# Side work spread over more gaps and over ScalarE, and one GpSimd addition made in two

## The chip, the cores and the metric
The kernel runs on one core of one Trainium2 chip. The metric is the device time of one execution in microseconds; the median of three runs of the kernel before is 1218.67 us (1215.61 to 1218.83).

## The reference, cut to what matters
Eight sequences of 512 tokens and 256 features go through a linear attention layer with a Taylor feature map, a residual and a layer norm, and then through a top-1 router with eight experts of width 1024 (GELU), a residual and a layer norm. All is float32.

```python
def taylor_exp(x):                       # 16 features -> 1 + 16 + 256
    x2 = (x[..., :, None] * x[..., None, :]).reshape(*x.shape[:-1], FD * FD) / R2
    return jnp.concatenate([jnp.ones_like(x[..., :1]), x / RRD, x2 / RD], axis=-1)
# 16 heads; q, k, v from x; k_enc, v_enc from the first 128 tokens
A_qk = jnp.tril(einsum('bhnd,bhmd->bhnm', taylor_exp(q), taylor_exp(k)))
y1 = einsum('bhnm,bhme->bhne', A_qk, v)
y2 = einsum('bhnm,bhme->bhne', einsum('bhnd,bhmd->bhnm', q_f, k_enc_f), v_enc)
z = 1.0 / ((q_f * k_state).sum(-1) + EPS)       # the row sum of the weights
x = layernorm(x + ((y1 + y2) * z) @ Wout.T)
# then: top-1 expert of softmax(x @ wr + br), gate, gelu(x @ w1 + b1) @ w2 + b2
x = layernorm(x + moe(x))
```

The weight of a query and a key is (s + sqrt(1/2))^2 + 1/2 of the scaled dot product s, so that one square and one addition of a half stand for the feature map.

## The kernel before, in words
The function `attention` handles the eight sequences (batches) one after the other, and each batch as eight pairs of heads. A pair has four units: the score blocks of unit 0 (encoder keys), 1, 2 and 3 (the causal key tiles). A batch is therefore 32 gaps, numbered g = 0 to 31, and each engine runs its own hand-written order over the gaps; semaphores tie them together.

In gap g with unit u = g % 4, for pair n = 8b + g // 4:

- TensorE multiplies the scores of pair n + 1, unit u (`scores`, L725, into two PSUM slots), then weighs the values of pair n with the finished weights of unit u (`weigh`, L746), in unit 3 also sums the row sums of the weights (`denominators`, L759). After that it does at most one *piece*, side work for the batch before or after, into the single PSUM bank `piece`: a V projection (L622, `V_LATE_AT` for the second half of this batch's values, `V_EARLY_AT` for the first half of the next batch's), a query or key projection for the next batch (`QK_AT`, five of them), an output projection of the batch before (`OUT_AT`, four, L669), the two turns of the normalised rows (`TURN_AT`, L705) and the router (`ROUTER_AT`, L712). A piece waits until the reader of the one ahead has emptied the bank (`piece_read`).
- ScalarE first copies the piece of gap g - 1 if it is a V piece (L392) or the high part of a QK piece (L404), then squares the scores (L379); in unit 0 it also adds a half (L384) and copies the attention output of the last pair (L412).
- VectorE first makes the low part of a QK piece (L482) or adds the residual (L530, L532) for the piece of gap g - 1, then finishes the weights of unit u of pair n + 1: a masked multiply (L490, for units 1 to 3) and an addition of a half to the rest (L493, called half-add below). Behind that stands its side work by gap number: the inversion of the row sums (gap 1, L497), the split of the next batch's x into a high part `xh` (gap 6, L470) and a low part `xl` (gap 7, L474), eight normalisations of the last batch's attention output (gaps 8 to 15, L502), moments (25, L537), centring (27, L542), the copies of the turned rows (L548) and the router's logits (L553).
- GpSimd adds the finished weights of the pair's blocks for the row sums: one addition of 2 x 512 columns after unit 1 (L339), one of 2 x 384 and one of 2 x 128 after unit 2 (L342, L345), one of 2 x 256 after unit 3 (L349). In gap 26 it makes `rstd` (L354, L357), for which the centring waits.
- SyncE's queue holds all loads and stores in a fixed order. It sends the high and low parts of q and k to DRAM (`send`, L209 to L218), gathers them as operands of two pairs (`gather`, L226, L229), stores the inverse row sums (L241), loads them spread over the partitions (`load_inverse`, L252, two pairs each), stores the rows (L257) and loads x.

The first projection of the next batch (`project_qk`, i = 0) waits for both parts of x (`x_split`); output projection 0 waits for all eight normalisations; turn 0 waits for all centred rows (`y_ready`). `experts` runs after the attention.

Of the kernel before, what the change touches and what calls it, by code (L numbers as in the profile page):

```python
# [11 lines left out]
ALU = mybir.AluOpType  # L12
# [26 lines left out]
V_LATE_AT = {0: 0, 1: 1, 2: 2, 3: 3, 4: 4}  # L39
QK_AT = {9: 0, 11: 1, 13: 2, 15: 3, 17: 4}  # L40
OUT_AT = {18: 0, 20: 1, 22: 2, 24: 3}
V_EARLY_AT = {19: 0, 21: 1, 23: 2, 25: 3, 27: 4}
TURN_AT, ROUTER_AT = {29: 0, 30: 1}, 31
XH_GAP, XL_GAP = 6, 7
INVERT_GAP, NORM_GAP, MOMENTS_GAP, CENTRE_GAP, RSTD_GAP = 1, 8, 25, 27, 26
# [53 lines left out]
def attention(nc, sem, xT_in, x_in, wqk_in, wv_in, wo_in, wr_in, br_in, ybuf, inv_rows, k_rows, q_rows,  # L99
              logits, ident, tables):  # L100
    falling, tile_starts, count128, before, ones, ones32 = tables
    with ExitStack() as ctx:
# [80 lines left out]
        def _(sp):  # L183
# [89 lines left out]
            for b in range(B):  # L273
                if b + 1 < B:
                    load_x(b + 1)
                if b > 0:
                    store_inverse(b - 1)
                gather(b, 2)
                if b > 0:
                    for g in range(PAIRS // 2):  # L280
                        load_inverse(b - 1, g)
                gather(b, 3)
                if b + 1 < B:
                    send(b + 1, 0)
                    gather(b + 1, 0)
                    send(b + 1, 1)
                if b > 0:
                    store_rows(b - 1)
                if b + 1 < B:
                    gather(b + 1, 1)  # L290
                if b > 0:
                    load_rows(b)
# [4 lines left out]
        def _(pool):  # L297
# [34 lines left out]
            def add_blocks(n, u):  # L332
                src, dst = w[:, n % 2, :, :], wsum[:, n % 2, :, :]
                pool.wait_ge(w_ready, FIXES * n + FIXED[u])
                if u == 1:
# [3 lines left out]
                    pool.tensor_tensor(dst, src[:, :, 0:N], src[:, :, N:2 * N], ALU.add).then_inc(wsummed, 1)  # L339
# [32 lines left out]
        def _(act):  # L372
# [32 lines left out]

            def copy_att(n):
                act.wait_ge(weighed, UNITS * (n + 1))
                if n == 0:
                    act.wait_ge(w_split, 22)
                if n >= ATT:  # L410
                    act.wait_ge(piece_full, nth((n - ATT) // PAIRS, "out", NT - 1) + 1)
                act.activation(att[:, n % ATT, :], osum[n % 2][:, :], ACT.Copy).then_inc(att_copied, 1)  # L412
# [19 lines left out]
            for b in range(B):  # L432
                for g in range(GAPS):
# [5 lines left out]
                    if b + 1 < B and g - 1 in V_EARLY_AT:  # L439
                        copy_values(b + 1, 0, V_EARLY_AT[g - 1])  # L440
                    if b * PAIRS + p + 1 < B * PAIRS:
# [6 lines left out]
            copy_att(B * PAIRS - 1)  # L448

        @block.vector  # L450
        def _(dve):
# [15 lines left out]
            def split_x_high(b):  # L467
                dve.wait_ge(xT_loaded, 16 * (b + 1))
                dve.wait_ge(piece_full, nth(b - 1, "v", 9) + 1)
                dve.tensor_copy(xh[:, :, :], xT[:, :, :]).then_inc(x_split, 1)  # L470

            def split_x_low(b):
# [72 lines left out]
            def copy_turned(b, k):  # L545
                dve.wait_ge(piece_full, nth(b, "turn", k) + 1)
                bank = osum[1] if b == B - 1 and k == 1 else piece
                dve.tensor_copy(yT[:, 4 * k:4 * k + 4, :],  # L548
                                bank[:, :].rearrange("p (t n) -> p t n", n=P)).then_inc(piece_read, 1)

# [25 lines left out]
            for b in range(B):  # L576
                for g in range(GAPS):
# [5 lines left out]
                    if b > 0 and g - 1 in TURN_AT:  # L583
                        copy_turned(b - 1, TURN_AT[g - 1])
                    if b > 1 and g == 0:
                        logits_of(b - 2)
                    if n < B * PAIRS and u > 0:
                        finish_weights(n, u)
                    if b + 1 < B and g == XH_GAP:
                        split_x_high(b + 1)  # L590
# [4 lines left out]
                    if b > 0 and 0 <= g - NORM_GAP < PAIRS:  # L595
                        normalise((b - 1) * PAIRS + g - NORM_GAP)
# [4 lines left out]
            logits_of(B - 2)  # L601
# [11 lines left out]
            copy_turned(B - 1, 0)  # L613
            copy_turned(B - 1, 1)
# [664 lines left out]
```

## Time and profile before
| | us |
|---|---|
| median of the runs | 1218.67 |
| the profiled execution, its own time | 1217.28 |
| its span | 1215.5 |
| TensorE busy | 1080.9 (89%) |
| VectorE busy | 627.7 (52%) |
| ScalarE busy | 495.5 (41%) |
| GpSimd busy | 592.4 (49%) |
| attention phase, to the last batch's row sums | about 798 |
| expert phase, to the end | about 417 |

The page of a profile gives busy time by engine, then 40 slices of the span, then groups of instructions by line. A share over the whole span says little here, as the two phases have different limits; the timelines of single stretches and the list of who waited for whom say more. "Idle before" in a timeline row is the time in which the engine had nothing to do ahead of that row, with what ended it. The granted clock is a share of 2.4 GHz; 0.50 is 1.2 GHz, and a value between is a mix of both over the stretch.

### The profile page before, as it was taken

Reading aid. Unit: us, or ns where it says so; the run is one execution under the profiler, and the core shown is the slowest. Engines: PE = TensorE matmul, PEld = TensorE weight load, DVE = VectorE, ACT = ScalarE, POOL = GpSimd, SP = SyncE. Lnnn points to the kernel's source line nnn. Section 1 sums busy time; section 2 is a strip of 40 time slices with the busy share of each in tenths; the row PEclk is TensorE's granted clock in tenths of the full one; section 3 lists DMA queues with packets and bytes.
Section 4 is the critical chain, followed back from the end, with each engine's and each line's share of the span. In section 5 each row is a group of like instructions: output and inputs, shape, how many; then the busy total and the mean of one; then the engine's idle time right before and its main releaser. Section 6 shows DMA issues by size and latency. Waiting matters only on the chain. (4 is left out here: it accounts for less than half of the span.)

```text
span 1215.5 us, 16762 instructions
## 1 busy us (share of the span) xinstructions
PE 1080.9 (89%) x5296; PEld 629.5 (52%) x5297; DVE 627.7 (52%) x986; ACT 495.5 (41%) x868; POOL 592.4 (49%) x571
## 2 busy tenths in 40 slices
PE   5789899999989989989998998883479999999994
PEld 4344455445436445445544543463357766677663
DVE  5476864583492574466448349646423334343342
ACT  2557554544553454454454455300023233332331
POOL 1467755573574565456457357500124544444442
PEclk9789999999999899999999998976589999999998
DMA  6635352443534235235244343014551000111010
GB/s 205 249 108 183 92 193 83 142 152 118 155 120 161 92 114 218 102 91 184 85 150 148 122 131 92 1 35 169 226 237 33 31 33 29 34 35 31 25 31 2
DMA packets 54110, 134.90 MB, mean 111 GB/s; under 512 B 5854, under 2 KB 10176, under 8 KB 51746
## 3 DMA queue, kind: packets, MB, share of 16 engines
q1 hardware_dynamic: 50306, 124.81, 29.7%
q0 software_dynamic: 3744, 9.31, 2.5%
q8 instruction: 35, 0.57, 0.2%
q14 instruction: 25, 0.20, 0.1%
HBM read 87.73 MB, written 47.29 MB: 111 GB/s over the span
## 5 line engine op out<-in xcount | busy, mean ns | idle before, releaser
L379 ACT ACTIVATE w<-slot 128x1024 f32<-128x1024 f32 (+1 forms) x256 | 233.4, 915 | 176.3 <-PE slot L725 173.6
L339 POOL TENSOR_TENSOR wsum<-w 128x1024 f32<-128x1024 f32 x64 | 158.9, 2483 | 258.6 <-DVE w L493 258.6
L490 DVE SCALAR_TENSOR_TENSOR w<-w,mask 128x256 f32<-128x256 f32 (+1 forms) x192 | 192.9, 1005 | 169.6 <-ACT w L379 158.9
L746 PE MATMUL osum<-w,values 128*64 128x512 f32 (+3 forms) x1280 | 264.1, 511 | 2.0 <-DVE w L493 1.9
L342 POOL TENSOR_TENSOR wsum<-wsum,w 128x768 f32<-128x768 f32 x64 | 126.6, 1978 | 59.6 <-DVE w L493 59.6
L1156 ACT ACTIVATE active<-upT,b 128x128 f32<-128x128 f32 x312 | 84.9, 383 | 158.4 <-PE upT L1234 158.4
L1210 PE MATMUL down<-w,active 128*128 x624 | 144.2, 385 | 2.5 <-ACT active L1156 2.5
L1222 PE MATMUL up<-w,rowsT 128*128 x312 | 143.3, 603 | 0.7 <-ACT rowsT L1145 0.7
L725 PE MATMUL slot<-qop,kop 64*128 64x512 f32 (+3 forms) x640 | 130.2, 438 | 10.5 <-issue 8.3
L493 DVE TENSOR_SCALAR w<-w 128x768 f32<-128x768 f32 (+2 forms) x192 | 138.8, 723 | 0.0
L1210 PEld LDWEIGHTS down<-w,active 128*128 128x128 f32 x624 | 117.6, 193 | 18.7 <-issue 3.8
L725 PEld LDWEIGHTS slot<-qop,kop 64*128 64x128 f32 x640 | 58.0, 195 | 132.1 <-issue 118.6
L349 POOL TENSOR_TENSOR wsum<-wsum,w 128x512 f32<-128x512 f32 x64 | 93.6, 1463 | 25.5 <-DVE w L493 24.0
L669 PE MATMUL piece<-wo,att 128*128 128x256 f32 x448 | 104.2, 385 | 1.6 <-DVE att L502 1.6
L669 PEld LDWEIGHTS piece<-wo,att 128*128 128x128 f32 x448 | 82.8, 190 | 31.5 <-ACT values L392 9.7
L746 PEld LDWEIGHTS osum<-w,values 128*64 128x64 f32 x1280 | 68.7, 142 | 57.0 <-issue 44.2
L1187 DVE COPY inner<-up 128x1024 f32<-128x1024 f32 x39 | 47.7, 1223 | 91.2 <-PE up L1222 91.2
L392 ACT ACTIVATE values<-piece 128x512 f32<-128x512 f32 x75 | 44.9, 598 | 113.3 <-PE piece L622 113.3
L1222 PEld LDWEIGHTS up<-w,rowsT 128*128 128x128 f32 x312 | 57.3, 194 | 58.8 <-issue 58.7
L1170 DVE TENSOR_TENSOR result<-down,b 128x256 f32<-128x256 f32 x39 | 16.6, 424 | 114.8 <-PE down L1210 87.3
L530 DVE TENSOR_TENSOR y<-piece,y 128x256 f32<-128x256 f32 x28 | 11.9, 424 | 115.2 <-PE piece L669 115.2
L384 ACT ACTIVATE w<-w 128x1024 f32<-128x1024 f32 x64 | 67.7, 1058 | 2.0
(186 smaller groups left out, 1215.9 us busy)
## 6 DMA issues: line engine op xcount, KB each, us to landing
kop<-k_rows SPq DMA_DIRECT2D x32, 640.0 KB, 4.7
qop<-q_rows SPq DMA_DIRECT2D x32, 512.0 KB, 5.9
w<-in_w SPq DMA_DIRECT2D x16, 1024.0 KB, 9.5
inv<-inv_rows SPq DMA_DIRECT2D x56, 256.0 KB, 5.7
k_rows<-kh SPq DMA_DIRECT2D x32, 320.0 KB
k_rows<-kl SPq DMA_DIRECT2D x32, 320.0 KB
q_rows<-qh SPq DMA_DIRECT2D x32, 256.0 KB
q_rows<-ql SPq DMA_DIRECT2D x32, 256.0 KB
```

Of the source, the lines that this page charges most:

```text
L339: pool.tensor_tensor(dst, src[:, :, 0:N], src[:, :, N:2 * N], ALU.add).then_inc(wsummed, 1)
L342: pool.tensor_tensor(dst[:, :, P:N], dst[:, :, P:N], src[:, :, 2 * N + P:3 * N], ALU.add).then_inc(wsummed, 1)
L349: pool.tensor_tensor(dst[:, :, 2 * P:N], dst[:, :, 2 * P:N], src[:, :, 3 * N:WIDTH], ALU.add).then_inc(wsummed, 1)
L379: act.activation(w[:, n % 2, :, at:at + cols], slot[u % 2][:, :, 0:cols], ACT.Square, bias=HALF_ROOT).then_inc(squared, 1)
L490: dve.scalar_tensor_tensor(src[:, :, 0:cut], src[:, :, 0:cut], 0.5, mask[:, 0:cut].unsqueeze(1).to_broadcast([P, 2, cut]), ALU.add, ALU.mu ...
L493: dve.tensor_scalar(src[:, :, cut:], src[:, :, cut:], 0.5, None, ALU.add).then_inc(w_ready, 1)
L669: last = pe.matmul(piece[:, 0:D], att[:, (b * PAIRS + p) % ATT, t * P:t * P + P], wo[:, p, :], start=(p == 0), stop=(p == PAIRS - 1))
L725: last = pe.matmul(slot[u % 2][:, s, col:col + N - q0], kop[HD * s:HD * s + HD, n % RING, j * P:j * P + P], qop[HD * s:HD * s + HD, n % RI ...
L746: last = pe.matmul(osum[n % 2][HD * s:HD * s + HD, q0:N], values[:, j, h * HD:h * HD + HD], w[:, n % 2, s, at:at + N - q0], start=(u == 0) ...
L1156: act.activation(active[:, k % 2, c, :], upT[:, c * P:(c + 1) * P], ACT.Gelu, bias=b1[:, bass.ds(e * IC + c, 1)]).then_inc(active_ready, 1)
L1210: last = pe.matmul(down[k % 2][:, :], active[:, k % 2, c, :], w2[:, bass.ds(e, 1), c, :].rearrange("p o d -> p (o d)"), start=(c == 0), st ...
L1222: last = pe.matmul(up[:, h * 512:(h + 1) * 512], rowsT[:, k % 2, c, :], w1[:, bass.ds(e, 1), c, h * 512:(h + 1) * 512].rearrange("p o d -> ...
```

## The change
The gaps of most pieces move. V pieces of this batch run in gaps 0, 1, 3, 5, 6; QK pieces in 10, 12, 14, 25, 27; outputs in 15, 17, 19, 21; V pieces of the next batch in 16, 18, 20, 22, 24; turns in 26 and 28; the router in 30. The normalisations go by a table, into gaps 4, 5, 6, 7, 9, 10, 12, 13; `xh` to gap 7 and `xl` to 8; moments to 22, `rstd` to 23, centring to 24. The split of `xh` and the two copies of turned rows move from VectorE to ScalarE, ahead of its square of the same gap. The logits are read in gap 31, not at the start of the next batch. In SyncE's queue two of the four inverse loads now stand ahead of the gather of pairs 4 and 5, and the store of the rows stands ahead of the second `send`. GpSimd's addition of 2 x 512 columns (L339) becomes two of 512, one for each head; the second one signals.

```diff
--- before.py
+++ after.py
@@ -36,13 +36,14 @@
 UNIT_AT, UNIT_COLS = [0, 512, 1024, 1536], [512, 512, 512, 256]
 FIXED, FIXES = [0, 2, 4, 6], 6
 RING, ATT, INV = 4, 14, 4
-V_LATE_AT = {0: 0, 1: 1, 2: 2, 3: 3, 4: 4}
-QK_AT = {9: 0, 11: 1, 13: 2, 15: 3, 17: 4}
-OUT_AT = {18: 0, 20: 1, 22: 2, 24: 3}
-V_EARLY_AT = {19: 0, 21: 1, 23: 2, 25: 3, 27: 4}
-TURN_AT, ROUTER_AT = {29: 0, 30: 1}, 31
-XH_GAP, XL_GAP = 6, 7
-INVERT_GAP, NORM_GAP, MOMENTS_GAP, CENTRE_GAP, RSTD_GAP = 1, 8, 25, 27, 26
+V_LATE_AT = {0: 0, 1: 1, 3: 2, 5: 3, 6: 4}
+QK_AT = {10: 0, 12: 1, 14: 2, 25: 3, 27: 4}
+OUT_AT = {15: 0, 17: 1, 19: 2, 21: 3}
+V_EARLY_AT = {16: 0, 18: 1, 20: 2, 22: 3, 24: 4}
+TURN_AT, ROUTER_AT = {26: 0, 28: 1}, 30
+XH_GAP, XL_GAP = 7, 8
+NORM_AT = {4: 0, 5: 1, 6: 2, 7: 3, 9: 4, 10: 5, 12: 6, 13: 7}
+INVERT_GAP, MOMENTS_GAP, CENTRE_GAP, RSTD_GAP = 1, 22, 24, 23
 COPY_UNIT, DEN_UNIT = 0, 3
 QH = N // 2
 
@@ -275,18 +276,21 @@
                     load_x(b + 1)
                 if b > 0:
                     store_inverse(b - 1)
+                if b > 0:
+                    for g in range(2):
+                        load_inverse(b - 1, g)
                 gather(b, 2)
                 if b > 0:
-                    for g in range(PAIRS // 2):
+                    for g in range(2, PAIRS // 2):
                         load_inverse(b - 1, g)
                 gather(b, 3)
                 if b + 1 < B:
                     send(b + 1, 0)
                     gather(b + 1, 0)
-                    send(b + 1, 1)
                 if b > 0:
                     store_rows(b - 1)
                 if b + 1 < B:
+                    send(b + 1, 1)
                     gather(b + 1, 1)
                 if b > 0:
                     load_rows(b)
@@ -336,7 +340,8 @@
                     pool.wait_ge(enc_ready, n + 1)
                     if n >= 2:
                         pool.wait_ge(den_full, n - 1)
-                    pool.tensor_tensor(dst, src[:, :, 0:N], src[:, :, N:2 * N], ALU.add).then_inc(wsummed, 1)
+                    pool.tensor_tensor(dst[:, 0, :], src[:, 0, 0:N], src[:, 0, N:2 * N], ALU.add)
+                    pool.tensor_tensor(dst[:, 1, :], src[:, 1, 0:N], src[:, 1, N:2 * N], ALU.add).then_inc(wsummed, 1)
                 elif u == 2:
                     pool.wait_ge(wsummed, 4 * n + 1)
                     pool.tensor_tensor(dst[:, :, P:N], dst[:, :, P:N], src[:, :, 2 * N + P:3 * N],
@@ -402,6 +407,17 @@
                 bank = first_bank[i] if b == 0 else piece[:, :]
                 src = bank[:, 0:2 * P].rearrange("p (m n) -> p m n", m=2) if i == 2 else bank
                 act.activation(dst, src, ACT.Copy, scale=CQ if i in (0, 3) else 1.0).then_inc(qk_hi, 1)
+
+            def split_x_high(b):
+                act.wait_ge(xT_loaded, 16 * (b + 1))
+                act.wait_ge(piece_full, nth(b - 1, "v", 9) + 1)
+                act.activation(xh[:, :, :], xT[:, :, :], ACT.Copy).then_inc(x_split, 1)
+
+            def copy_turned(b, k):
+                act.wait_ge(piece_full, nth(b, "turn", k) + 1)
+                bank = osum[1] if b == B - 1 and k == 1 else piece
+                act.activation(yT[:, 4 * k:4 * k + 4, :], bank[:, :].rearrange("p (t n) -> p t n", n=P),
+                               ACT.Copy).then_inc(piece_read, 1)
 
             def copy_att(n):
                 act.wait_ge(weighed, UNITS * (n + 1))
@@ -438,6 +454,10 @@
                         high_qk(b + 1, QK_AT[g - 1])
                     if b + 1 < B and g - 1 in V_EARLY_AT:
                         copy_values(b + 1, 0, V_EARLY_AT[g - 1])
+                    if b > 0 and g - 1 in TURN_AT:
+                        copy_turned(b - 1, TURN_AT[g - 1])
+                    if b + 1 < B and g == XH_GAP:
+                        split_x_high(b + 1)
                     if b * PAIRS + p + 1 < B * PAIRS:
                         square(b * PAIRS + p + 1, u)
                         if u == 0:
@@ -446,6 +466,8 @@
                         copy_att(b * PAIRS + p - 1)
                 copy_den(b)
             copy_att(B * PAIRS - 1)
+            copy_turned(B - 1, 0)
+            copy_turned(B - 1, 1)
 
         @block.vector
         def _(dve):
@@ -464,12 +486,8 @@
                 dve.wait_ge(w_split, 6 + 2 * (4 * c + n) + 1)
                 dve.tensor_tensor(lo, src, hi.bitcast(F32), ALU.subtract).then_inc(w_split, 1)
 
-            def split_x_high(b):
+            def split_x_low(b):
                 dve.wait_ge(xT_loaded, 16 * (b + 1))
-                dve.wait_ge(piece_full, nth(b - 1, "v", 9) + 1)
-                dve.tensor_copy(xh[:, :, :], xT[:, :, :]).then_inc(x_split, 1)
-
-            def split_x_low(b):
                 dve.wait_ge(x_split, 2 * b + 1)
                 dve.tensor_tensor(xl[:, :, :], xT[:, :, :], xh[:, :, :].bitcast(F32), ALU.subtract).then_inc(x_split, 1)
 
@@ -541,12 +559,6 @@
                 for t in range(NT):
                     dve.tensor_scalar(y[:, t, :], y[:, t, :], mv[:, t, 0:1], rstd[:, t:t + 1], ALU.subtract,
                                       ALU.mult).then_inc(y_ready, 1)
-
-            def copy_turned(b, k):
-                dve.wait_ge(piece_full, nth(b, "turn", k) + 1)
-                bank = osum[1] if b == B - 1 and k == 1 else piece
-                dve.tensor_copy(yT[:, 4 * k:4 * k + 4, :],
-                                bank[:, :].rearrange("p (t n) -> p t n", n=P)).then_inc(piece_read, 1)
 
             def logits_of(b):
                 dve.wait_ge(piece_full, nth(b, "router", 0) + 1)
@@ -580,25 +592,20 @@
                         low_qk(b + 1, QK_AT[g - 1])
                     if b > 0 and g - 1 in OUT_AT:
                         residual(b - 1, OUT_AT[g - 1])
-                    if b > 0 and g - 1 in TURN_AT:
-                        copy_turned(b - 1, TURN_AT[g - 1])
-                    if b > 1 and g == 0:
-                        logits_of(b - 2)
+                    if b > 0 and g - 1 == ROUTER_AT:
+                        logits_of(b - 1)
                     if n < B * PAIRS and u > 0:
                         finish_weights(n, u)
-                    if b + 1 < B and g == XH_GAP:
-                        split_x_high(b + 1)
                     if b + 1 < B and g == XL_GAP:
                         split_x_low(b + 1)
                     if b > 0 and g == INVERT_GAP:
                         invert(b - 1)
-                    if b > 0 and 0 <= g - NORM_GAP < PAIRS:
-                        normalise((b - 1) * PAIRS + g - NORM_GAP)
+                    if b > 0 and g in NORM_AT:
+                        normalise((b - 1) * PAIRS + NORM_AT[g])
                     if b > 0 and g == MOMENTS_GAP:
                         moments(b - 1)
                     if b > 0 and g == CENTRE_GAP:
                         centre(b - 1)
-            logits_of(B - 2)
             invert(B - 1)
             pick(0)
             pick(1)
@@ -610,8 +617,6 @@
                 residual_last(t)
             moments(B - 1)
             centre(B - 1)
-            copy_turned(B - 1, 0)
-            copy_turned(B - 1, 1)
             logits_of(B - 1)
 
         @block.tensor
```

## Rows read from the trace of the kernel before
**Rows 1.** The page, part 1: busy time, share of the span, instructions.
```profile
PE 1080.9 (89%) x5296; PEld 629.5 (52%) x5297; DVE 627.7 (52%) x986; ACT 495.5 (41%) x868; POOL 592.4 (49%) x571
```
**Rows 2.** Waits of TensorE, 0 to 760 us: us in total, times, longest.
```profile
PE piece L622 <- DVE xl L474: 22.6, 7, 4.0
PE piece L705 <- DVE y L542: 11.5, 6, 1.9
...
PE piece L622 <- DVE ql L482: 8.1, 6, 1.4
```
**Rows 3.** Timeline of TensorE, 340 to 410 us: start, duration, what, [idle before, releaser].
```profile
342.17 0.70 PE L622 MATMUL piece<-xh,wqk_h 128*128 128x512 f32 x2 [3.09 <-DVE xl L474]
...
363.12 0.74 PE L622 MATMUL piece<-xh,wqk_h 128*128 128x512 f32 x2 [1.36 <-DVE ql L482]
...
406.80 0.63 PE L705 MATMUL piece<-ident,y 128*128 128x128 f32 x4 [1.92 <-DVE y L542]
```
**Rows 4.** Windows, one batch: length, busy by engine, granted clock, DMA share, GB/s.
```profile
412.95:512.39 99.44, 93.05 (x490) 49.01 (x490) 56.19 (x85) 48.95 (x65) 54.77 (x35) 0.95 0.39 132
```
**Rows 5.** Windows behind four idle times of TensorE, same columns.
```profile
342.00:348.00 6.00, 5.83 (x32) 2.90 (x32) 5.80 (x8) 2.22 (x3) 3.90 (x2) 0.72 0.26 78
363.00:369.00 6.00, 5.88 (x31) 4.23 (x32) 3.35 (x6) 1.52 (x2) 4.21 (x3) 1.00 0.53 209
506.00:512.00 6.00, 5.78 (x35) 2.92 (x36) 4.56 (x8) 1.62 (x2) 4.08 (x2) 0.72 0.84 284
512.00:518.00 6.00, 6.00 (x27) 3.76 (x28) 1.30 (x3) 2.95 (x4) 2.15 (x3) 0.72 0.45 176
```
**Rows 6.** Timeline of TensorE: a V piece, gaps without pieces, an output piece.
```profile
330.12 0.73 PE L622 MATMUL piece<-wv_h,xh 128*128 128x512 f32 x2
...
331.72 0.50 PE L725 MATMUL slot<-qop,kop 64*128 64x512 f32 x2
...
337.57 0.50 PE L725 MATMUL slot<-qop,kop 64*128 64x512 f32 x2
...
382.55 3.72 PE L669 MATMUL piece<-wo,att 128*128 128x256 f32 x16
```
**Rows 7.** Timeline of VectorE, 334 to 344 us.
```profile
334.81 2.44 DVE L490 SCALAR_TENSOR_TENSOR w<-w,mask 128x512 f32<-128x512 f32 x1 [0.55 <-ACT w L379]
...
338.12 2.04 DVE L490 SCALAR_TENSOR_TENSOR w<-w,mask 128x256 f32<-128x256 f32 x1
...
340.81 1.21 DVE L474 TENSOR_TENSOR xl<-xT,xh 128x1024 fp32r<-128x1024 f32 x1
341.94 1.77 DVE L502 TENSOR_TENSOR att<-att,inv 128x512 f32<-128x512 f32 x1
```
**Rows 8.** Timeline of GpSimd, 328 to 344 us.
```profile
328.38 1.28 POOL L349 TENSOR_TENSOR wsum<-wsum,w 128x512 f32<-128x512 f32 x1 [0.23 <-DVE w L493]
334.35 2.36 POOL L339 TENSOR_TENSOR wsum<-w 128x1024 f32<-128x1024 f32 x1 [4.69 <-DVE w L493]
...
340.97 2.20 POOL L349 TENSOR_TENSOR wsum<-wsum,w 128x512 f32<-128x512 f32 x1 [0.23 <-DVE w L493]
```
**Rows 9.** SyncE's timeline; then DMA issues: KB, us to landing, 340:346 and 327.5:329.4.
```profile
323.73 1.30 SPq L241 DMA_DIRECT2D inv_rows<-den_sb  x4
...
327.09 26.16 SPq L252 DMA_DIRECT2D inv<-inv_rows  x8
...
inv<-inv_rows SPq DMA_DIRECT2D x2, 256.0 KB, 3.7
...
inv<-inv_rows SPq DMA_DIRECT2D x4, 256.0 KB, 7.7
```
**Rows 10.** Timeline of ScalarE: a 1024-column square.
```profile
339.17 1.02 ACT L379 ACTIVATE w<-slot 128x1024 f32<-128x1024 f32 x1
```
**Rows 11.** Timeline of VectorE: the centring.
```profile
404.33 2.33 DVE L542 TENSOR_SCALAR y<-y,mv,rstd 128x256 f32<-128x256 f32 x4 [1.96 <-POOL rstd L357]
```
**Rows 12.** Timeline of TensorE, last batch: turn 0.
```profile
792.40 1.09 PE L705 MATMUL piece<-ident,y 128*128 128x128 f32 x4 [6.04 <-DVE y L542]
```

## The prediction
> **What bounds the kernel now.** I read the busy shares first: TensorE is busy 89% of the span and no other engine is near [rows 1]. The attention phase is eight batches, to about 800 us; the expert phase behind it is untouched by the diff, so only the batches can move. Next the waits of TensorE in that phase [rows 2]: it waits on VectorE's `xl` before the first projection of every next batch, on the centred `y` before the rows are turned, and on `ql` before the last projection. The timeline gives them for one batch: 3.09, 1.36 and 1.92 us [rows 3], 6.4 us of a batch of 99.44 us whose mean clock is 0.95 [rows 4]. The clock windows show what else an idle costs: behind the 3.09 us idle the grant is 0.72 over 6 us (1.7 us lost), behind a 1.9 us idle at the turn 0.72 over 12 us (3.4 us lost), behind the 1.36 us idle 1.00 [rows 5]. The two levels are 1.2 and 2.4 GHz. So a batch is 88 us of matmul work, 6.4 us of idle and 5 us of clock; the last two are what the change can touch.
>
> **Unit lengths.** Four gaps with no piece take 337.57 - 331.72 = 5.85 us, 1.46 each; a V or QK piece 331.72 - 330.12 = 1.6 us; an output piece 3.7 [rows 6]. Sixteen gaps, five V and three QK pieces are 36.2 us.
>
> **How VectorE and GpSimd delay each other.** A mask multiply (L490) of unit 2 issued at 334.81 lasts 2.44 us: it ends 0.54 us after GpSimd's 128x1024 addition (334.35 + 2.36 = 336.71). The one at 338.12 waits in the same way. Then `xl` (340.81) runs 1.21 us, GpSimd's 512-column addition issued at 340.97 takes 2.20 instead of 1.28, and the normalisation issued at 341.94 ends 0.54 us after it [rows 7, 8]. I take this as: one holder at a time, the one that asked first is next. The Trainium skill, "SBUF — State Buffer", section "Who interferes with whom", says the shared pair is an exclusive lock held for the whole instruction and that issue order decides who blocks; by that rule, the trace agrees.
>
> **Part 1, the addition in two.** 1024 columns cost 2.36, 512 cost 1.28 [rows 8]: twice 1.28 and some 0.08 between them is 0.28 more for each of 64 pairs, 18 us of GpSimd time, which has idle time beside most pairs. The waiting mask multiply of unit 2 gets the port after 1.28 instead of 2.36, but the second half has then asked before VectorE's next operation, so that waits 1.28 again: multiply 1.28 + 0.54, second half 1.28, half-add tail 0.3 makes 3.4 us from the start, against 2.36 + 0.54 + 0.35 = 3.25 today. I take 0 for it where VectorE is the late one (bounds: +0.3, and -1.2 if VectorE's next operation slips in before the second half). The Trainium skill, "GPSIMD Engine Reference", section "Performance versus the Vector engine", speaks against it: more dispatch for every GpSimd instruction than VectorE's roughly 0.16 us; 64 more by that figure would be at least 10 us if nothing hid them, an estimate from the page.
>
> **Part 2, the inverse in front.** Normalisations now start in gap 4, not 8. The chain in the batch that starts at 316.45: the stores go out 323.73 to 325.03, the first inverse load was issued at 327.09 at the latest possible moment for the stores' landing [rows 9]. In the new queue it no longer stands behind a gather, so 326.5 to 327.1, its twin 0.6 later, landing 3.7 us after issue as it does when alone [rows 9]: 331 to 331.4. VectorE reaches this wait at about 328.3 and stands; behind it is queued unit 1 of gap 5, whose squares come at 331.25 anyway (V pieces in gaps 1, 3, 5 shift it). So almost nothing lost. The gather moved behind goes out near 329.5 and is wanted in gap 12, 346: covered. Without cover each us late counts in full.
>
> **Part 3, `xl`.** V pieces in gaps 3, 5, 6 and QK in 10 instead of 9: TensorE wants `xl` at 316.45 + 11 x 1.46 + 5 x 1.6 = 340.55. `xh` goes to ScalarE in gap 7 (1.02 us for 1024 columns [rows 10]), which is idle half the time; the square behind it ends at 336.95, before TensorE needs the slot at 337.6. VectorE from 331.4: unit 1 and normalisation 1 to 332.9; first half addition to 334.1, multiply 334.65, second half 335.9, half-add 336.2, normalisation 2 336.8; addition of 768 to 338.55, multiply 338.85, addition of 256 to 339.6, half-add 339.85, normalisation 3 340.45; addition of 512 to 341.7, then `xl` 342.85. Idle 2.45 against 3.09: four normalisations now stand ahead of it, which eats most of the extra slack. **QK1:** TensorE wants it at 347.6 (some 349 with the slow clock); unit 1, normalisation 4, the two halves round unit 2, normalisation 5 and `ql` end at 348.95. Idle up to 1.5, in the place of clock loss. **Output 0** now follows QK2 directly (gaps 14, 15): by the same steps `kl` of QK2 is read at 358.5, wanted at 356.55: idle 2.0 (0.75 if VectorE slips in). So output 0 starts at 358.6, 42.15 us into the batch for 36.2 us of work.
>
> **Part 4, the second half.** 52.4 us of work follow (four outputs, five V, two QK, turns, router, 16 gaps). At the turn VectorE still waits for GpSimd's `rstd`, 1.96 us today [rows 11], but a V and a QK piece now lie between: `y` is ready some 1.4 us before TensorE asks. Late next are the low parts of QK3 (0.35) and QK4 (0.7), each read one gap before a turn. The turn's copies go to ScalarE: two of 0.6 us; the squares behind them are wanted two units later. `store_rows` before the second `send` costs nothing (rows are centred before QK3 is sent), and the second gather lands 5 us before gap 4 of the next batch. Logits one gap earlier: nothing. So 53.5 us, and if the 2.0 us idle costs clock like the 3.09 one, 1.9 more: 42.15 + 53.5 + 1.9 = 97.6 against 99.4.
>
> **Sum.** Six full batches: 6 x -1.8 = -10.7. Batch 0 (no normalisations, `xl` waits 4.0 [rows 2]): -1.1. Last batch: it is bound by the VectorE and GpSimd loop in the middle (output 0 comes 2.5 us earlier for the same work), and its 6.04 us wait at the turn [rows 12] becomes 3.8 with a slower end: -4.4 together. -16.2 from the profiled 1217.28 (span 1215.5) is 1201; the median of the runs is 1218.67, 1.4 higher, so about 1203.
>
> **Rivals.** (a) The same mechanism better: VectorE's half-add slips in before the second half, or output 0's idle of about 2 us costs no clock, as the 1.36 one does not. 1.7 to 3 us more for each of six batches: 1187 to 1192. For: one idle of nearly that length was free; against: the order of asking in rows 7, 8 gives the port to GpSimd. (b) **Slower: the inverse loads come late.** A load beside other traffic lands after 7.7 us, not 3.7 [rows 9]: normalisation 0 then ends near 335.5, and since it stands in VectorE's queue ahead of the weights of gap 5 and of `xl`, the whole chain to output 0 is 3.4 us later in seven batches: +24 on -16, 1226. It decides from 2.3 us of lateness, that is a landing after 333.7. For: half a MB each and a second group right behind; against: the gather that made those loads slow now stands behind them. (c) The idles only change place: low parts read one gap before the next piece (QK2, QK3, QK4) cost 1 us each more than I worked out, nothing in the trace shows such tight spacing on a full VectorE: 1213 to 1222. (d) The split does nothing and the rest is as forecast: 1203, no separate time.
>
> **Chances.** Forecast 1203 (1194 to 1212): 0.45. (a) 0.22. (c) 0.18, two thirds of it within the bound of 0.3%. (b) 0.15. A change of 0.3% (3.7 us) is about what a measurement of this kernel can tell from none. Faster 0.68, the same 0.13, slower 0.19. The range takes in (a) and most of (c): 1188 to 1222.
>
> **What would show it.** Right: TensorE's waits on `xl` near 2.4 us a batch, none on `y` in the full batches, new ones on `kl` before output 0; batches of 97 to 98 us; multiplies of unit 2 at 1.3 to 1.8 us instead of 2.4 to 2.9 in dense pairs, with the half-add behind them near 1.6. Wrong: VectorE idle in gap 4 past 331.4 on the inverse (b); TensorE waiting on the low parts before both turns for over 1 us (c); clock 1.00 after output 0 (a). If `xl` waits as long as before while the batch shrinks, part 3 was wrong and part 4 carried it.

## The result: 3% less, more than twice the forecast gain

| | before | changed |
|---|---|---|
| median, us | 1218.22 | 1180.26 |
| ratio, 95% interval | | 0.9706 [0.9668, 0.9744] |
| profiled execution, us (span) | 1217.28 (1215.5) | 1180.28 (1178.5) |

The forecast was 1203 with a range of 1188 to 1222. The direction held; the time lies 8 us below the range. Run 12 is a second measurement of the changed kernel. It gave 0.9714 [0.9693, 0.9734].

First the waits of TensorE from 60 to 740 us in the changed kernel, which answer to [rows 2] (us in total, times, longest):

```profile
PE piece L627 <- DVE xl L492: 19.3, 7, 4.9
PE piece L674 <- DVE kl L500: 5.3, 6, 1.1
PE piece L627 <- DVE ql L500: 2.6, 3, 1.1
```

The wait on `y` is gone in all full batches, the one on `xl` has hardly changed, and a smaller one on `kl` stands before output 0. The batch from 309 us in TensorE's timeline, which answers to [rows 3]; between the second row and the end of the batch there is no idle at all (QK pieces are now L627, outputs L674, turns L710, the router L717, the batch starts at 309.03):

```profile
336.17 0.70 PE L627 MATMUL piece<-xh,wqk_h 128*128 128x512 f32 x2 [3.02 <-DVE xl L492]
...
350.42 3.72 PE L674 MATMUL piece<-wo,att 128*128 128x256 f32 x16 [0.75 <-DVE kl L500]
...
390.67 0.66 PE L710 MATMUL piece<-ident,y 128*128 128x128 f32 x4
```

The whole of that batch, and the windows behind the two idles and around the turns, with the columns of [rows 4, 5] (the clock is the third value from the end):

```profile
309.16:402.81 93.65, 89.89 (x490) 47.21 (x490) 57.69 (x81) 50.55 (x68) 57.19 (x43) 0.98 0.44 140
...
336.17:342.17 6.00, 6.00 (x27) 2.38 (x27) 6.00 (x8) 2.06 (x3) 4.90 (x3) 0.72 0.50 148
350.42:356.42 6.00, 6.00 (x26) 4.11 (x27) 3.36 (x4) 1.78 (x2) 3.55 (x3) 1.00 0.49 162
389.66:401.66 12.00, 12.00 (x82) 6.50 (x82) 7.99 (x10) 7.62 (x12) 7.73 (x7) 1.00 0.52 166
```

Behind the 3.0 us idle the clock falls to 0.72 as before. Behind the 0.75 us one it is 1.00, and so it is around turns and router, where the kernel before had 0.72 for 12 us.

One batch does not fit this picture. In batch 1, the first with normalisations, the inverse is late and the batch gains nothing:

```profile
135.58 0.69 DVE L520 TENSOR_TENSOR att<-att,inv 128x512 f32<-128x512 f32 x1 [5.27 <-DMA inv<-inv_rows]
...
147.03 1.19 PE L627 MATMUL piece<-xh,wqk_h 128*128 128x512 f32 x2 [4.90 <-DVE xl L492]
...
117.68:216.21 98.53, 92.55 (x490) 48.46 (x490) 61.67 (x82) 50.68 (x67) 59.22 (x44) 0.95 0.42 136
```

Normalisation 0 starts 18.0 us into this batch (it begins at 117.55), against 14.7 to 15.7 in the other five full ones.

**Where the 37 us of the profiled executions come from.** I divided both traces at ScalarE's copy of the row sums, once a batch. Batch 0: -1.6. The six full batches: 591.5 to 566.6, and as one router (1.95) now falls into them that fell behind their end before, -26.9. All of it comes from five of them; batch 1 is 0.6 longer for the same work (98.5, against 96.0 and the router). The last batch: 87.3 to 79.3, -8.0 (83.8 in the profile of run 12, with more lost clock). The rest, less that router: -0.5. For the five full batches with the same borders I split the length into work (the rest: TensorE at full clock), idle, and clock lost (length times one minus the mean grant, taken from the trace before rounding):

| mean of five batches, us | length | work | idle | clock lost |
|---|---|---|---|---|
| before | 99.1 | 87.9 | 6.4 | 4.8 |
| changed | 93.6 | 88.2 | 4.0 | 1.4 |

Of 5.5 us a batch, 2.4 are idle and 3.4 are clock; the work is the same to 0.3. Two kinds of slow stretch went. Rows at half the clock (0.50), with the router of the same batch:

```profile
408.31:411.72 3.41, 3.41 (x14) 1.30 (x10) 2.46 (x4) 1.27 (x2) 2.44 (x2) 0.50 1.01 333
412.43 1.95 PE L712 MATMUL piece<-wr,yT 128*128 128x8 f32 x16
415.13:418.55 3.42, 3.42 (x9) 1.84 (x6) 0.00 (x0) 2.29 (x3) 0.00 (x0) 0.50 0.01 2
```

Each costs 1.7 us. In the kernel before, one starts 0.2 to 1.5 us behind the start of turn 0 in all six full batches, and a second one 1.8 to 2.7 us behind the start of the router in four of the six. The changed kernel's profile has neither.

### The profile page after: what moved, and what is told of

Its sections match the earlier page's. It is cut to its first block and busy times, and to the rows that moved or that the text cites. A ratio compares the mean times of both kernels' runs of the same rounds, so it can differ in the third digit from the quotient of the medians.

```text
span 1178.5 us, 16833 instructions
## 1 busy us (share of the span) xinstructions
PE 1063.4 (90%) x5296; PEld 621.4 (53%) x5297; DVE 634.1 (54%) x963; ACT 508.0 (43%) x891; POOL 613.0 (52%) x635
## 5 line engine op out<-in xcount | busy, mean ns | idle before, releaser
L751 PE MATMUL osum<-w,values 128*64 128x512 f32 (+3 forms) x1280 | 253.6, 492 | 5.7 <-DVE w L511 5.7
L508 DVE SCALAR_TENSOR_TENSOR w<-w,mask 128x256 f32<-128x256 f32 (+1 forms) x192 | 175.8, 916 | 150.8 <-ACT w L384 138.0
L343 POOL TENSOR_TENSOR wsum<-w 128x512 f32<-128x512 f32 x64 | 95.7, 1496 | 222.7 <-DVE w L511 222.7
L511 DVE TENSOR_SCALAR w<-w 128x768 f32<-128x768 f32 (+2 forms) x192 | 189.4, 986 | 0.0
L730 PE MATMUL slot<-qop,kop 64*128 64x512 f32 (+3 forms) x640 | 126.6, 426 | 9.8 <-issue 7.2
L674 PE MATMUL piece<-wo,att 128*128 128x256 f32 x448 | 105.5, 389 | 5.7 <-DVE kl L500 5.3
L674 PEld LDWEIGHTS piece<-wo,att 128*128 128x128 f32 x448 | 83.8, 192 | 34.2 <-ACT values L397 9.7
L751 PEld LDWEIGHTS osum<-w,values 128*64 128x64 f32 x1280 | 65.4, 136 | 58.5 <-issue 43.3
L344 POOL TENSOR_TENSOR wsum<-w 128x512 f32<-128x512 f32 x64 | 94.1, 1470 | 0.0
L354 POOL TENSOR_TENSOR wsum<-wsum,w 128x512 f32<-128x512 f32 x64 | 86.9, 1358 | 12.2 <-DVE w L511 7.7
```

The lines of the kernel that those rows point to most:

```text
L343: pool.tensor_tensor(dst[:, 0, :], src[:, 0, 0:N], src[:, 0, N:2 * N], ALU.add)
L344: pool.tensor_tensor(dst[:, 1, :], src[:, 1, 0:N], src[:, 1, N:2 * N], ALU.add).then_inc(wsummed, 1)
L354: pool.tensor_tensor(dst[:, :, 2 * P:N], dst[:, :, 2 * P:N], src[:, :, 3 * N:WIDTH], ALU.add).then_inc(wsummed, 1)
L508: dve.scalar_tensor_tensor(src[:, :, 0:cut], src[:, :, 0:cut], 0.5, mask[:, 0:cut].unsqueeze(1).to_broadcast([P, 2, cut]), ALU.add, ALU.mu ...
L511: dve.tensor_scalar(src[:, :, cut:], src[:, :, cut:], 0.5, None, ALU.add).then_inc(w_ready, 1)
L674: last = pe.matmul(piece[:, 0:D], att[:, (b * PAIRS + p) % ATT, t * P:t * P + P], wo[:, p, :], start=(p == 0), stop=(p == PAIRS - 1))
```

## The experiments

All ratios are to the kernel before, on the same chip. "Clock lost at the turn" is taken from 6 us before turn 0 to 17 us behind it, in six full batches, from the grant before rounding.

**1. The split alone.**

```diff
-pool.tensor_tensor(dst, src[:, :, 0:N], src[:, :, N:2 * N], ALU.add).then_inc(wsummed, 1)
+pool.tensor_tensor(dst[:, 0, :], src[:, 0, 0:N], src[:, 0, N:2 * N], ALU.add)
+pool.tensor_tensor(dst[:, 1, :], src[:, 1, 0:N], src[:, 1, N:2 * N], ALU.add).then_inc(wsummed, 1)
```

> Kernel before with the addition of 2 x 512 columns made in two, nothing else. Theory A (the gain comes from the turn: its idle and the slow clock behind it): the split gives VectorE nothing where VectorE is late, since the second half takes the port before VectorE's next operation; ratio to before 0.998 to 1.003, the idles on xl 3.1, on ql 1.35 and on y 1.9 us a batch stay. Rival B (the split frees VectorE): xl idle falls by about 1 us and more, ratio 0.985 to 0.99.

0.9998 [0.998, 1.0017]. VectorE's timeline at the place of [rows 7], and GpSimd's two halves:

```profile
335.12 1.36 DVE L491 SCALAR_TENSOR_TENSOR w<-w,mask 128x512 f32<-128x512 f32 x1 [0.54 <-ACT w L380]
336.40 1.50 DVE L494 TENSOR_SCALAR w<-w 128x512 f32<-128x512 f32 x1
...
334.65 1.27 POOL L339 TENSOR_TENSOR wsum<-w 128x512 f32<-128x512 f32 x1 [4.55 <-DVE w L494]
335.89 1.73 POOL L340 TENSOR_TENSOR wsum<-w 128x512 f32<-128x512 f32 x1
```

The half-add in the kernel before:

```profile
337.18 0.41 DVE L493 TENSOR_SCALAR w<-w 128x512 f32<-128x512 f32 x1
```

The multiply waits 1.1 us less than in [rows 7] and the half-add behind it 1.1 us longer: from the multiply's issue to the end of the half-add it is 2.78 us in both kernels (334.81 to 337.59 before). In these rows the port goes to whoever asked first: the multiply, issued during the first half, ends 0.56 us behind it, the second half (335.89) comes before the half-add (336.40), and the half-add ends 0.28 us behind the second half.

**2. The changed kernel without the split** (the diff of 1 reversed).

> The changed kernel with the addition of 1024 columns in one again. Theory A: 0.970 of before as the changed kernel, within 0.3%, xl idle again 2 to 3 us. Rival B: 10 to 20 us of the 38 are lost, ratio 0.978 to 0.987.

0.9693 [0.9657, 0.9729]. The split does nothing that either run can tell (run 1 bounds it at 0.2%); the gain comes from the new order and the move to ScalarE. Its profile held something I had not looked for. Around the router of one batch TensorE has no idle to speak of, and still:

```profile
292.60:301.70 9.10, 8.99 (x56) 3.91 (x52) 5.65 (x8) 6.53 (x10) 5.08 (x4) 1.00 0.49 158
301.77:311.77 10.00, 10.00 (x48) 5.20 (x48) 5.83 (x6) 4.39 (x7) 6.86 (x4) 0.66 0.86 299
```

The router starts at 301.77; the half clock begins at 303.73 and lasts 6.8 us.

**3. The kernel before, with one piece put between output 3 and turn 0.**

```diff
-QK_AT = {9: 0, 11: 1, 13: 2, 15: 3, 17: 4}
+QK_AT = {9: 0, 11: 1, 13: 2, 15: 3, 26: 4}
```

> Kernel before with one piece moved: the last QK projection from gap 17 to gap 26, between the last output and turn 0. Theory A: 1.6 us more of TensorE work lies between the last output and turn 0, so the 1.9 us idle on y falls to 0 to 0.7 and the 0.72 clock of the 12 us behind it (3.4 us) goes; the 1.35 us idle on ql goes as well. 4.5 to 6 us for each of six batches: 1182 to 1192, ratio 0.970 to 0.979. Rival C (the clock is not tied to the idle): 1.9 + 1.35 for each of six, 1199, ratio 0.984.

0.9925 [0.9901, 0.995]: about 9 us (6 to 12), not 27 to 36. The idle on `y` fell to 0.3 and that on `ql` went, as expected. But VectorE's copies of the turned rows, which the wait on `y` had hidden, now kept turn 1 and the router waiting (TensorE's waits, 60 to 800 us):

```profile
PE piece L622 <- DVE xl L474: 21.0, 7, 3.1
PE piece L705 <- DVE y L542: 7.7, 7, 6.0
PE piece L712 <- DVE yT L548: 7.2, 6, 1.2
...
PE piece L705 <- DVE yT L548: 2.0, 6, 0.3
```

(6.0 of the second row is the last batch.) The idle in the stretch is 1.8 us instead of 1.9, and it loses 3.4, 1.7, 3.4, 1.7, 3.4, 1.7 us of clock, where before the change it was 3.4, 1.7, 3.4, 3.4, 3.4, 1.7. So a long wait on one thing is not needed. This left two readings: any 2 us of idle in this stretch, or turns and router standing close together.

**4. The changed kernel with turns and router close together.**

```diff
-TURN_AT, ROUTER_AT = {26: 0, 28: 1}, 30
+TURN_AT, ROUTER_AT = {28: 0, 29: 1}, 30
```

> The changed kernel with turn 0 in gap 28 and turn 1 in 29, just ahead of the router in 30, as close together as before the change; y is ready long before. Theory F (the slow clock behind the turn comes from the turns and the router standing close, pieces with few columns for each instruction, not from the idle on y): without any idle on y the stretch behind the router loses clock again in most of the six full batches, 1.6 to 3.5 us each; with some wait for the copies 1190 to 1205, ratio 0.977 to 0.988. Theory A (it came from the idle): the clock stays at 1.00 there, ratio 0.969 to 0.973.

0.9703 [0.9672, 0.9733], clock lost at the turn 0, 0, 1.7, 0, 0, 1.7 with 0.1 us of idle, the same as run 12 shows without this edit. Theory F, that closeness is the cause, falls.

**5. Only the idle at the turn given back.**

```diff
-INVERT_GAP, MOMENTS_GAP, CENTRE_GAP, RSTD_GAP = 1, 22, 24, 23
+INVERT_GAP, MOMENTS_GAP, CENTRE_GAP, RSTD_GAP = 1, 22, 25, 23
```

> The changed kernel with the centring in gap 25, behind the weights of that gap, and nothing else moved: this gives back only the idle on y before turn 0. It ran at 9.7 us behind output 3, turn 0 asks at 12.1; behind the weights it ends near 12.5 to 13.5, so an idle of 0.5 to 1.5 us and more for the low part of QK3 behind it, 1.5 to 2.5 together. Theory A2 (what slows the clock behind the turn is some 2 us of idle within that stretch, whoever causes it): loss of 1.6 to 3.5 us in most batches on top, 3 to 5 us for each of six batches: 1198 to 1210, ratio 0.983 to 0.993. If the clock doesn't answer: only the idle, 1189 to 1195.

0.989 [0.9862, 0.9918], 22 us slower than the changed kernel. VectorE and TensorE there:

```profile
393.92 3.29 DVE L560 TENSOR_SCALAR y<-y,mv,rstd 128x256 f32<-128x256 f32 x4
397.13 0.68 DVE L500 SCALAR_TENSOR_TENSOR ql<-piece,qh 128x512 fp32r<-128x512 f32 x1
...
397.86 0.66 PE L710 MATMUL piece<-ident,y 128*128 128x128 f32 x4 [1.80 <-DVE ql L500]
```

TensorE waits so in all six full batches. Clock lost at the turn: 1.7, 1.7, 0, 1.7, 1.7, 0. In each of the four the half clock begins 0.7 to 1.5 us behind the start of turn 0, where no full batch of a profile without an idle there has it, and not behind the router:

```profile
495.90:499.31 3.41, 3.41 (x17) 1.70 (x14) 1.98 (x2) 0.59 (x2) 3.10 (x3) 0.50 0.56 147
```

Of the 22 us, 17.4 lie in the six full batches of the profile: 12.3 us more idle, 10.8 of them at the turn, and 5.1 more of lost clock. Against the profile of run 12 it is 16.7, split nearly the same. So one gap of VectorE's order, with a centring that runs beside GpSimd's additions (3.29 us against 1.38), gives back more than half of the gain.

**6. Two projections behind the turns instead of between.**

```diff
-QK_AT = {10: 0, 12: 1, 14: 2, 25: 3, 27: 4}
+QK_AT = {10: 0, 12: 1, 14: 2, 27: 3, 29: 4}
```

> The changed kernel with the last two QK projections behind the turns (gaps 27 and 29), so that one piece less lies between output 3 and turn 0. The prediction's reason (a V and a QK piece between cover the wait on y) would have turn 0 ask 1.6 us earlier, 10.5 us behind output 3. Theory H (the chain to y itself became 2.6 us shorter, as rstd now runs behind the 512-column addition and the centring beside an idle GpSimd): y is ready at 9.7, no idle on y, 1178 to 1184. If the cover was the reason: an idle of about 0.5 to 1.5 us on y in six batches and 1188 to 1200.

0.9886 [0.9855, 0.9918]. On the point it was made for, theory H held: turn 0 asks 10.55 us behind output 3 (386.51 to 397.06) and does not wait, since the centring, begun at 394.78 and 1.38 us long, ends 9.65 us behind it.

```profile
394.78 1.38 DVE L560 TENSOR_SCALAR y<-y,mv,rstd 128x256 f32<-128x256 f32 x4 [2.66 <-POOL rstd L362]
...
397.06 0.66 PE L710 MATMUL piece<-ident,y 128*128 128x128 f32 x4
...
403.11 0.66 PE L710 MATMUL piece<-ident,y 128*128 128x128 f32 x4 [0.89 <-DVE ql L500]
```

On the time I was wrong by 20 us: turn 1 waits for the low part of QK3, and the inverse comes late. Its store is issued as early as in the changed kernel (7.3 us into the batch in both), but now runs beside the gather, which is issued at 314.59 to 317.51 (4 us before the batch in the changed kernel) and moves 1.15 MB, and SyncE waits 5.0 us for it to land instead of 1.9. VectorE then stands 7.0 us instead of 4.4 at normalisation 0, and the idle on `xl` grows (27.2 us in seven batches against 19.3):

```profile
332.70 0.69 DVE L520 TENSOR_TENSOR att<-att,inv 128x512 f32<-128x512 f32 x1 [7.00 <-DMA inv<-inv_rows]
...
344.12 1.19 PE L627 MATMUL piece<-xh,wqk_h 128*128 128x512 f32 x2 [5.08 <-DVE xl L492]
```

This is what the prediction's rival (b) feared, a late inverse ahead of the whole chain, though through its store and not through its loads.

**7. Most of the router left out** (in the first seven batches 14 of its 16 matmuls, so three of four tiles have no logits).

```diff
-                for t in range(NT):
+                for t in range(NT if b == B - 1 else 1):
```

> The changed kernel with two of the router's 16 matmuls in the first seven batches; the other 14 are left out, so the logits of three tiles of four are not computed and tokens go to other experts. Theory F: no loss of clock behind the router in any batch (before this edit it comes in some executions and batches with no idle near it); time 7 x 1.65 = 11.5 us of work less, and less spread between executions: 1165 to 1170. If the router is no trigger, some batches still lose 1.6 or 3.2 us at the turn.

No clock lost at the turn in any of six batches, as expected of the router as the trigger. By itself this shows little, as the first profile of the changed kernel has none either. What points at the router is where the losses lie: the seven profiles of changed order with the whole router and next to no idle at the turn (the result and runs 2, 4, 9, 10, 11, 12) have one in 16 of 42 full batches, and all 16 begin 1.8 to 3.7 us behind the start of the router, with at most 0.13 us of idle in the 9 us ahead. One from run 12:

```profile
395.80 1.95 PE L717 MATMUL piece<-wr,yT 128*128 128x8 f32 x16
...
398.30:401.71 3.41, 3.41 (x18) 0.78 (x14) 3.16 (x4) 1.82 (x3) 3.19 (x3) 0.50 1.02 296
```

The time stayed: 0.9688 [0.9659, 0.9717], 1178.75 us, with 11.5 us of matmul work gone. In batches 2 to 6 normalisation 0 now starts 15.6 to 17.3 us into the batch, not 14.7 to 15.7, the idle on `xl` rose to 25.4 us (seven times), and 1.7 to 5.1 us of clock a batch were lost. The first half of a batch is set by the inverse and VectorE's chain behind it, not by TensorE.

**8. `xh` and the copies back on VectorE.** The activations in `split_x_high` and `copy_turned` become `dve.tensor_copy` in VectorE's order at the same gaps.

> The changed kernel with xh and the copies of the turned rows made on VectorE again. Theory: VectorE works without a pause from normalisation 0 to the low part of QK2, so 0.6 us for xh comes later at output 0 in seven batches and the copies (0.69 each) delay the low part of QK4 by some; 0.5 to 1.5 us a batch, 1184 to 1190, ratio 0.972 to 0.977. Rival G (the offload to ScalarE is the main gain): 1195 or more.

0.9783 [0.9762, 0.9804]: the move to ScalarE is worth about 9 us, the upper end of what I gave it. Rival G falls. The idle on `xl` is 3.45 us in the batch shown, and VectorE's copy of turn 0 keeps the piece behind it, QK4, waiting:

```profile
336.69 0.70 PE L627 MATMUL piece<-xh,wqk_h 128*128 128x512 f32 x2 [3.45 <-DVE xl L486]
...
393.62 0.73 PE L627 MATMUL piece<-xh,wqk_h 128*128 128x512 f32 x2 [0.30 <-DVE yT L480]
```

**9. Normalisation 3 behind `xl`.**

```diff
-NORM_AT = {4: 0, 5: 1, 6: 2, 7: 3, 9: 4, 10: 5, 12: 6, 13: 7}
+NORM_AT = {4: 0, 5: 1, 6: 2, 9: 3, 10: 4, 11: 5, 12: 6, 13: 7}
```

> The changed kernel with normalisation 3 to 5 in gaps 9 to 11, so that none stands between the weights of gap 7 and xl. Theory A: xl is issued before GpSimd's 512-column addition asks for the port, 0.7 + 1.3 us earlier; its idle falls from 2 to 3 us to 0.3 to 1.2 and the clock behind it stays at 1.00; 2 to 3 us for each of seven batches, less 0.5 for later low parts: 1163 to 1170, ratio 0.955 to 0.961. Rival D (the low parts behind are late instead, as the normalisations must go somewhere): idles on ql and kl grow by as much, ratio 0.968 to 0.972.

0.9717 [0.9683, 0.9752]. The idle on `xl` falls from 19.3 to 8.1 us in total, that on `ql` rises from 2.6 to 11.9. Rival D was right: the same work in another order on the engine that sets the pace.

**10. Normalisations from gap 5.**

```diff
-NORM_AT = {4: 0, 5: 1, 6: 2, 7: 3, 9: 4, 10: 5, 12: 6, 13: 7}
+NORM_AT = {5: 0, 6: 1, 7: 2, 8: 3, 9: 4, 10: 5, 12: 6, 13: 7}
```

> The changed kernel with normalisation 0 in gap 5, behind the weights of that gap, and the first four in 5 to 8. In the changed kernel VectorE stands 4.4 us at normalisation 0 until the inverse has landed, while the squares of gap 5 are ready about 1.5 us earlier. Theory: the weights of gap 5 are made in that time; xl comes some 3 us earlier and its idle is under 0.5, output 0 1.0 to 1.5 us earlier, idle on ql 1 to 2.5 instead; 1.0 to 1.5 us for each of seven batches, 1169 to 1175, ratio 0.959 to 0.965. Rival (normalisations later crowd the low parts, as in the run with normalisation 3 behind xl): 0.969 to 0.973.

0.9668 [0.9644, 0.9693]. What helps here is that VectorE makes the weights of gap 5 while the inverse is still on its way; in this batch there is no wait on the inverse left:

```profile
315.59 0.42 DVE L508 SCALAR_TENSOR_TENSOR w<-w,mask 128x256 f32<-128x256 f32 x1 [3.54 <-ACT w L384]
315.93 0.55 DVE L511 TENSOR_SCALAR w<-w 128x768 f32<-128x768 f32 x1
316.40 0.69 DVE L520 TENSOR_TENSOR att<-att,inv 128x512 f32<-128x512 f32 x1
```

Idle on `xl` 11.1, on `ql` 7.5. The gain over the changed kernel is half of what I expected: 5 to 6 us. Its interval lies at or below that of the second measurement (run 12), but overlaps the wider one of the first. In the profile the full batches 2 to 6 are no shorter than in the changed kernel (468.0 and 468.1 us): in the batch shown the weights start only 0.8 us before the normalisation. Batch 1, where the inverse comes at 18.0 us, goes from 98.5 to 93.6; its weights of gap 5 start 2.7 us before the inverse.

**11. As 10, and the half-add of unit 3 on ScalarE.** `square` of unit 3 is followed by an activation that adds a half to its unmasked columns and counts a semaphore of its own, for which the weighing and GpSimd's last addition wait; VectorE leaves that half-add out.

> Normalisations from gap 5 as in the run before, and the half-add of unit 3 (2 x 128 columns) on ScalarE, straight behind its square. Theory: output 0 is set by VectorE's unbroken chain from gap 5 to the low part of QK2, in which the half-add of unit 3 stands 0.8 us in each of three pairs, most of it waiting for GpSimd's port; 1.5 to 2.4 us earlier for seven batches, and less waiting in the last batch: 1158 to 1166, ratio 0.951 to 0.958. Rival (GpSimd's additions become the bound of the loop): 0.962 to 0.967.

0.9657 [0.9636, 0.9678], 1176.91 us: the rival's number. VectorE's saved half-add turns into a longer wait of the normalisation behind it for GpSimd's port (1.22 us instead of 0.68), so output 0 is not earlier:

```profile
325.17 1.22 DVE L527 TENSOR_TENSOR att<-att,inv 128x512 f32<-128x512 f32 x1
```

It is the fastest kernel of the study together with 10, from which it can't be told.

**12. The changed kernel again.**

> The changed kernel itself once more, with more rounds, as the measure for the small differences (normalisations from gap 5: 0.967 of before; with the half-add on ScalarE: 0.966; turns together: 0.970). If those gains of 3 to 5 us are real it stays at 0.969 to 0.972; if they are chance of the clock it comes to 0.966 to 0.968. In the profile: no idle at the turns, xl 2 to 3 us, and slow clock behind the router in none to three of six batches.

0.9714 [0.9693, 0.9734], clock lost at the turn 0, 0, 1.7, 0, 0, 1.7. Against this measurement the small gains of 10 and 11 are real.

## Why the prediction was wrong in size, step by step

**Bound and unit lengths.** Right: about 88 us of work a batch in both traces.

**Part 1, the split: 0.** Right, and by the mechanism given; runs 1 and 2 show it from both sides.

**Part 2, the inverse: landing at 331 to 331.4, that is 14.5 to 15 us into the batch, nearly free.** It began at 14.7 to 15.7 in five full batches (324.71 against 309.03 in the one shown). Near enough: run 10 shows that only 0.8 us of weights could have been made in that wait. In batch 1 it was wrong: 18.0 us, later than the bound that rival (b) gives (333.7, that is 17.25), and run 6 shows the same at 2.5 us more in the batch shown.

**Part 3, idle of 2.45 on `xl`, up to 1.5 before QK1, 2.0 before output 0; output 0 at 42.15 us.** Measured 3.02 (2.0 to 3.1 in five of the full batches, 4.9 in batch 1), 0 to 1.1, and 0.7 to 1.1; output 0 at 41.4 us. In the batch shown the chain through VectorE and GpSimd was worked out to within 1 us over twelve gaps. What the slow clock takes behind `xl` it gives back as less idle before QK1 and output 0, which the forecast saw for QK1.

**Part 4, the second half of the batch: 53.5 + 1.9 us. This step failed**; measured 52.25 in the batch shown (350.42 to 402.67), in two terms:

- Low parts of QK3 and QK4, 1.05 us: measured 0. The prediction shows no working for it; the one length of a centring in its rows is the 2.33 us of [rows 11], which ran beside GpSimd's 512-column addition, and behind the addition it took 1.38. VectorE was a microsecond further on, and the low part of QK3 was read at 390.60 for a turn that asked at 390.67. The margin was luck: run 5 moves the centring by one gap and pays 1.80 us.
- 1.9 us of clock behind output 0: measured 0 in all six full batches, after idles of 0.7 to 1.1, not 2.0.

Together with part 3's 0.75 these are 3.7 of the 4 us by which the batch shown (97.6 forecast, 93.65 measured) came out shorter. The other full batches but batch 1 are like it, 3.7 us a batch more than the gain of 1.8 that was forecast, 18.5 us for five; batch 1 takes 2.4 back. That makes 16.1 of the 20.7 us by which the profiled execution (1201 forecast, 1180.28 measured) was missed; the last batch has 3.6, the two ends the rest.

**The reason given for the idle on `y`** ("a V and a QK piece now lie between") was incomplete. Two V pieces lay there before too; what the change adds is one QK piece. Run 3 adds just that to the kernel before and leaves 0.3 us of the wait. Run 6 takes it away from the changed kernel and there is still no wait on `y`, so a second cause does as much. The chain from output 3 to a centred `y` had itself become 2.6 us shorter, 9.65 against 12.3 (394.35 to 406.66 before): `rstd` no longer starts behind the two additions of unit 2, and the centring has GpSimd's port free.

**The clock.** The forecast tied each loss to the idle ahead of it: 3.4 at the turn for 1.9 us of idle. Half of that reading was wrong: the second window of that pair in [rows 5], from 512, is the one behind the router. The 1.7 us right behind turn 0 go with the idle (six of six full batches before, four of six in run 5, none of 42 without it). The other 1.7 us come behind the router, in four of six batches before and in 16 of 42 without idle. That the changed kernel's profile has none of these is partly luck: over the seven profiles they cost 0 to 1.9 us a batch, 0.8 on average. Run 3 fits this, as its idle lies right in front of the router; run 4 excludes closeness. What decides whether a given router, or a given idle of 1.8 us, is followed by a slow stretch stays open.

**Last batch: -4.4.** Measured -8.0. The waits ahead of its output 0 came to 3.3 us where 5.3 stood before, and the lost clock to 3.4 where it was 6.8, though in the profile of run 12 it is 8.5. Its idle at the turn became 2.37, not 3.8 ([rows 12] had 6.04); the shorter centring probably has a part in this, which no run isolates:

```profile
754.49 0.63 PE L710 MATMUL piece<-ident,y 128*128 128x128 f32 x4 [2.37 <-DVE y L560]
```

**The rivals.** (a), the same mechanism better, is what happened (no clock lost behind output 0), and its range of 1187 to 1192 was still too careful, because it let only one of the terms improve at a time. (b) happened in one batch of seven: batch 1 is 4.9 us longer than the mean of the five behind it. (c) did not happen: `kl` before output 0 and `ql` before QK1 are its only traces. The range was too narrow below: each batch had three unknowns of 1 to 2 us, and in five of six all fell on the same side.

## What to carry to other kernels

- Before sizing a stall in a periodic schedule, write each batch as work at full clock + idle + lost clock. Here more than half of the gain of a batch was lost clock, and a 1.8 us idle given back cost 2.9 a batch, 0.85 of it clock. Do it for every batch: one of them behaved otherwise.
- When two engines share a port, take the duration of an operation from a row in which the other engine does what it will do after the change. Splitting the long operation only moved the wait by one instruction here, as its second half asked first.
- Where one engine works without a pause through a stretch, look for less work on it or an earlier start (run 8; run 10, in the batch with the late inverse). Another order on it (run 9) and less work on the engine that waits (run 7) gained nothing here.

## What the runs showed of the hardware that I had not expected

- The clock can fall to 1.2 GHz with TensorE busy throughout: in run 2 a grant of 0.66 over the 10 us from the start of a router of 16 matmuls of 8 columns, with 0.1 us of idle in the 9 us ahead of it. The 16 such falls all begin 1.8 to 3.7 us behind a router's start.
- An idle of 1.9 us on `y` was followed by a slow stretch in six of six batches, while in the two profiles of the changed kernel idles of 2.0 to 2.4 us on `xl` cost no clock and those of 2.5 to 3.1 cost none, 1.7 or 3.4 us.
- Most losses come in steps of 1.7 us, and the same batch of the same kernel shows different ones in two executions (0, 0, 0, 0, 0, 0 and 0, 0, 1.7, 0, 0, 1.7 at the turn in the two profiles of the changed kernel). It is the likely source of the 7 us between the executions of the changed kernel (1179.96 to 1187.22, mean clock 0.950 and 0.939).
- A centring takes 1.7 to 2.4 times its own time beside GpSimd's additions: its four operations took 1.38 us with GpSimd idle, 2.33 beside one addition of 512 columns (the kernel before) and 3.29 beside two (run 5).
- A small store took longer to land beside a gather of 1.15 MB: SyncE waited 5.0 us for the inverse's (run 6) and 1.9 where the gather had been issued earlier.
